# Adding x1 at the end of slot 3 of each step instead of in the middle of slot 4

## The reference

```
x1  = x + softmax(q k^T / 8) v @ Wo + bo      q = layernorm(x) @ Wq, 16 heads of 64;  k, v from the context
out = x1 + fp4(h) @ fp4(w_down)^T             h = silu(g) * u;  g, u = fp4(layernorm(x1)) @ fp4(w_gate, w_up)^T
```

## Time and profile before

| | |
|---|---|
| median of 3 runs | 984.9 us (982.71 to 985.96) |
| the profiled execution's own time | 986.75 us |
| its span, first to last instruction | 984.9 us |
| mean granted TensorE clock | 0.973 of full speed |
| PE busy | 857.0 us, 87% of the span |
| DVE busy | 757.5 us, 77% |
| ACT, POOL busy | 534.0 and 529.5 us, 54% each |
| steps between two adds of x1, away from setup | 24.7 us and 26.4 us in turn |

### The profile page before, as it was taken

How to read it: one execution, slowest core, us unless ns; L and a number is a source line. 1 busy time by engine, 2 the same in 40 slices (tenths; PEclk the granted TensorE clock), 3 DMA queues, 4 the chain that set the end, 5 groups by cost and what they waited for, 6 DMA issues and landing times.

```text
span 984.9 us, 21389 instructions
## 1 busy us (share of the span) xinstructions
PE 857.0 (87%) x6254; PEld 812.8 (83%) x6254; DVE 757.5 (77%) x2176; ACT 534.0 (54%) x1879; POOL 529.5 (54%) x677
## 2 busy tenths in 40 slices
PE   4786789999999999989989999989999999999874
PEld 3666789988888998888978888889888888888863
DVE  5857788877778888867878888876877888887762
ACT  4454455556565555556555555556555555655520
POOL 2545666554535656545554656554553656555651
PEclk9888999999999999999999999999999999999986
DMA  7101000001010000001000000001000000000000
GB/s 215 39 11 49 7 17 13 22 13 44 7 33 17 13 23 11 21 14 39 12 28 23 12 22 12 21 8 33 23 7 23 12 18 12 16 11 12 7 11 11
DMA packets 19869, 23.13 MB, mean 23 GB/s; under 512 B 2642, under 2 KB 18234, under 8 KB 19770
## 3 DMA queue, kind: packets, MB, share of 16 engines
q1 hardware_dynamic: 19770, 21.94, 7.2%
HBM read 17.74 MB, written 4.19 MB: 22 GB/s over the span
## 4 chain that ended last, share of the span: by engine, by line
PE 63%; DVE 21%; issue 8%; ACT 4%; POOL 2%; DMA 1%; DVEq 1%; SPq 0%; POOLq 0%; ACTq 0%
PE ps_g L1015 10%; PE ps_q L937 8%; PE ps_s L975 8%; PE ps_t L985 5%; PE ps_o L998 5%; PE ps_o L1000 5%; PE ps_o L999 5%; DVE negmax L782 3%; DVE pT_lo L637 3%; PE ps_m L865 3%; PE ps_g L900 3%; PE ps_m L1025 3%; PE ps_m L1027 2%; PE ps_m L1026 2%; DVE scales L667 2%
## 5 line engine op out<-in xcount | busy, mean ns | idle before, releaser
L472 POOL TENSOR_TENSOR probs<-probs,rsum 128x308 f32<-128x308 f32 x256 | 180.0, 703 | 284.2 <-DVE rsum L746 283.6
L610 ACT ACTIVATE probs<-ps_s,negmax 128x154 f32<-128x154 f32 x512 | 194.7, 386 | 229.4 <-DVE negmax L782 228.2
L998 PE MATMUL ps_o<-B_sb,pT_lo 128*128 128x256 f32 x640 | 183.6, 287 | 38.5 <-DVE x_both L804 33.9
L782 DVE TENSOR_REDUCE negmax<-ps_s 128x2 f32<-128x308 f32 x256 | 121.3, 474 | 78.4 <-PE ps_s L975 76.6
L1000 PE MATMUL ps_o<-B_sb,pT_hi 128*128 128x256 f32 x640 | 181.2, 283 | 0.0
L999 PE MATMUL ps_o<-B_sb,pT_hi 128*128 128x256 f32 x640 | 180.9, 283 | 0.0
L998 PEld LDWEIGHTS ps_o<-B_sb,pT_lo 128*128 128x128 f32 x640 | 121.7, 190 | 45.3 <-issue 42.9
L637 DVE TENSOR_TENSOR pT_lo<-ps_t,pT_hi 128x256 fp32r<-128x256 f32 (+1 forms) x256 | 122.7, 479 | 42.6 <-ACT pT_hi L514 37.4
L985 PE MATMUL ps_t<-ident,probs 128*128 128x128 f32 x640 | 115.0, 278 | 35.9 <-DVE pT_lo L637 35.3
L1015 PE MATMUL ps_g<-WGU,xqT_hi 128*128 128x352 f32 x512 | 136.6, 349 | 3.5 <-DVE B_sb L637 1.9
L514 ACT ACTIVATE pT_hi<-ps_t 128x256 fp32r<-128x256 f32 (+1 forms) x256 | 111.4, 435 | 29.1 <-PE ps_t L985 22.7
(11 more groups left out here) (149 smaller groups left out, 2236.7 us busy)
## 6 DMA issues: line engine op xcount, KB each, us to landing
xa<-in_x_dram SPq DMA_DIRECT2D x33, 128.0 KB, 2.1
xr<-in_x_dram SPq DMA_DIRECT2D x32, 128.0 KB, 2.0
out_dram<-y_xn SPq DMA_DIRECT2D x32, 128.0 KB, 1.7
W_sb<-in_L_xattn_Wk_dram SPq DMA_DIRECT2D x4, 512.0 KB, 4.4
W_sb<-in_L_xattn_Wv_dram SPq DMA_DIRECT2D x3, 512.0 KB, 3.6
probs<-in_L_xattn_Wq_dram SPq DMA_DIRECT2D x1, 1024.0 KB, 7.0
Wo_sb<-in_L_xattn_Wo_dram SPq DMA_DIRECT2D x1, 1024.0 KB, 6.6
VT<-in_ctx_dram SPq DMA_DIRECT2D x1, 384.0 KB
```

Of the source, the lines that this page charges most:

```text
L472: pool.tensor_tensor(unit, unit, rsum[:, 2 * u:2 * u + 2].unsqueeze(2) .to_broadcast([P, 2, M]), ALU.mult).then_inc(norm_p, 1)
L610: ins = act.activation(probs[:, h, 0:M], ps_s[k % 2][:, s * M:(s + 1) * M], ACT.Exp, bias=negmax[:, h:h + 1], accum_out=sums[:, h:h + 1])
L782: dve.tensor_reduce(negmax[:, 2 * k:2 * k + 2], ps_s[k % 2][:, 0:UM].rearrange("p (h m) -> p h m", h=2), AX_X, ALU.max, negate=True).then_ ...
L998: pe.matmul(ps_o[:, 0:C], lo[:, j, :], w[:, 0:C], start=first, stop=False)
```

## The change

DVE's add moves from the middle of slot 4 to the end of slot 3, with its three waits. The statistics of `x1` stay in slot 4. ACT's copy of the older `x1` to `y`, for which the add waits, moves from the end of slot 3 to the end of slot 2. PE, POOL and SP have the same instructions in the same order as before.

```diff
@@ ACT, step
                     if turn_at(t, k, 0) is not None:
                         chunk_hi(turn_at(t, k, 0))
-                    if down and k == 3:
+                    if down and k == 2:
                         at = pair - 2 + par
                         act.wait_ge(x1_v, d + 1)
                         if some(at):
...
@@ DVE, step
                     if before and k == 4:
-                        dve.wait_ge(o_mm, PAIRS * (e + 1))
-                        dve.wait_ge(xr_p, e + 1)
-                        if some(d + 1):
-                            dve.wait_ge(y_a, d + 1)
-                        elif not some(e):
-                            dve.wait_ge(raw_mm, RAW_T[3])
-                        dve.tensor_tensor(x1[1 - par], xr[1 - par][:, :], ps_o[:, 0:C], ALU.add).then_inc(x1_v, 1)
                         if some(e):
                             dve.wait_ge(xln2_a, e)
                         stats(x1[1 - par], st2, mv2, ve2, nm2, (x1_v, e + 1), ln2_v, 5 * e)
...
                         dve.wait_ge(xq_v, 6 * e + 3)
                         dve.tensor_scalar(xri[:, :], xri[:, :], TIES_DOWN, None, ALU.mult).then_inc(xq_v, 1)
+                    if before and k == 3:
+                        dve.wait_ge(o_mm, PAIRS * (e + 1))
+                        dve.wait_ge(xr_p, e + 1)
+                        if some(d + 1):
+                            dve.wait_ge(y_a, d + 1)
+                        elif not some(e):
+                            dve.wait_ge(raw_mm, RAW_T[3])
+                        dve.tensor_tensor(x1[1 - par], xr[1 - par][:, :], ps_o[:, 0:C], ALU.add).then_inc(x1_v, 1)
                     if gate and k == 6:
                         dve.wait_ge(h_v, Q * (f + 1))
```

## The result

The kernel after takes 944.5 us (median of 4 runs, 943.8 to 946.3); the kernel before, measured beside it, 983.9 us (4 runs, 982.7 to 986.0). The ratio is 0.960, with a 95% interval of 0.958 to 0.962. The forecast was 949 us in a range of 943 to 961, with 0.91 on faster: right in sign and range, 4.5 us too cautious. Of these, 1.0 is the kernel before, which the forecast took at 984.9 us; the medians differ by 39.4 us. The profiled execution took 946.30 us (span 944.4), against 986.75 us before: 40.45 us less, where 35.8 were forecast.

A forecast was written before the change was run, and what follows sets the result against it. PE (slots 2 to 5) and DVE (slot 5 to slot 1) bound the kernel in turn. Gains of 12 x 1.0 + 12 x 1.2 + 6 x 1.5 + 0.4 = 35.8 us off 984.9 gave 949 us, range 943 to 961.

The forecast's parts named there:

- The bound: PE and DVE bound the kernel in turn; PE's waits for the add of x1 make 38.5 us, 3.9% of the span.
- The add hidden: At the end of slot 3, DVE's idle of 0.30 + 0.52 + 0.26 us hides the 0.41 us add in odd steps.
- The copy at 0: ACT's copy of x1, moved a slot ahead, costs 0, with at most 0.4 us in 3 steps.
- PE's freed wait: PE's whole 1.32 us wait plus about 0.2 us goes: ahead by about 1.5 us in odd steps, 1.2 us in even.
- DVE's side of the odd step: DVE can follow by 0.52 us (statistics earlier), 0.30 (idle at slot 5's `negmax`) and up to 0.2: 1.0 us taken.
- What is late next: PE's gain lasts only as far as DVE follows; its slot 7 wait for `pT_lo` grows from 35 to 45 to 50 us.
- The clock: A half-clock stretch of PE, costing about 1.7 us, can appear or vanish; two either way are 3.4 us.
- The split of the distances: Distances between successive adds would be 23.7 and 25.2 us in turn.
- B: Rival: POOL holds the add on DVE by about 1.0 us, 9 us over 31 steps: 958 us, chance 0.05.
- C: Rival: DVE's or ACT's chain behind slot 4 takes back all but 0.44 us a step: 971 us, chance 0.13.
- D: Rival: DVE stands in slot 3 for PE's last `attend` product, each step 0.5 us longer: 1000 us, chance 0.05.
- E: Rival: the add still comes too late for PE, or another of `attend`'s waits ended last: 985 us, chance 0.04.

The follow-up runs named there:

- its version with the norm moved: Kernel after, with ACT's second layer norm moved ahead of slot 5's exponentials instead of behind them: 930.9 us (925.0 to 933.3), ratio 0.946.

## Why the prediction was right, and what was off

**The bound, right.** PE's waits for the add were on the path that sets the end: the add alone gives the whole gain, the copy alone none. It was read from two rows side by side: DVE stands idle ahead of the maximum, and PE stands idle behind it.

**The add hidden, right.** 0.67 us to spare in the odd step was forecast; one add more (0.44 us) costs nothing and three more cost 0.3 us there. In the even step, for which only the wait for `o_mm` had its room worked out (0.39 us), one more is free too.

**The copy at 0, right.** Both alone and taken back it changes no step by more than 0.04 us, but for the ones named with those runs. Where it stands only decides whether DVE's idle time is spent ahead of the add or behind it.

**PE's freed wait, right.** The 0.2 us above the bare wait (a shorter first product and its start) is borne out by the even steps: 0.99 + 0.2 was forecast, 1.19 to 1.24 us measured in 9 of 12. In "roll" steps 1.54 + 0.2 = 1.74 against 1.77 to 1.79: there I had put down the bare wait, about 1.5 us, and left the 0.2 out. That term was 0.8 us too small in all.

**DVE's side of the odd step, the mechanism right and the size too small.** This is the step that was mis-sized most: 12 x 1.0 forecast, 14.6 us measured. The working was 0.52 us (statistics earlier) + 0.30 (idle ahead of `negmax` of slot 5) + "up to 0.2". What is missing there shows beside one more row of DVE's timeline before, which stands between two of the earlier trace rows:

```profile
600.13 0.56 DVE L637 TENSOR_TENSOR hqT_lo<-ps_m,hqT_hi 128x384 fp32r<-128x384 f32 x1
```

Start to start, `negmax` of slot 4 to the statistics took 1.24 us before (596.78 to 598.02) and 0.73 after: 0.51 us. Statistics to `pT_lo` took 1.72 and now 1.50: 0.22 us. `pT_lo` to `negmax` of slot 5 took 1.25 and now 0.79: 0.46 us, where I had counted the 0.30 in the bracket. In sum 1.19 us. The bracket counts from the recorded end of the instruction before, but an instruction that needn't wait starts before that end: now `negmax` starts at 576.19, 0.47 us behind the start of `hqT_lo`, which is recorded for 0.55. So behind an idle of 0.30 stand 0.38 us or a little more; the other 0.07 us is `hqT_lo` itself, which started 0.39 us behind `pT_lo` and now starts 0.32 behind it. The Trainium skill (Perfetto Trace Analysis, Optimizing Scalar/DVE Operations) gives a DVE instruction a data-access overhead of about 60 ns on SBUF and 125 ns on PSUM, and says that the profiled latency has about twice that, since the write-acknowledgement half overlaps with the next instruction. That such starts overlap, these rows show, and their 0.08 us lies between the page's two figures.

**What is late next, right in place, the figure too high.** PE's wait for `pT_lo` was to grow to 45 to 50 us; it is 41.9. That range didn't follow from the prediction's own step, 0.7 to 1.2 us in 12 odd steps, which makes 41.3. The odd step now has 0.36 + 0.69 = 1.05 us, since DVE gained more than I gave it.

**The clock, in the bounds and not in the sum.** 1.6 us came from it. It can't be put down to the change: kernels with the same steps have the stretch in other places, and the executions of one kernel differ too (last section).

**The split of the distances, wrong without consequence.** 23.7 and 25.2 us between adds were forecast, 24.3 and 24.4 measured. The sum was forecast at 48.9 and is 48.7. The add's place within its step moved by different amounts in odd and even steps, and that enters both distances with opposite sign.

**The rivals.** B (POOL holds the add) is out: the add takes 0.41 us at 571.30, while POOL is at work on `hn`:

```profile
570.79 1.39 POOL L447 TENSOR_TENSOR hn<-hn,scales 128x704 f32<-128x704 f32 x1
```

The rule on two SBUF inputs that stood beside this step in the prediction (the Trainium skill, GPSIMD Engine Reference, Specifications) thus agrees with the trace in the new place too. C (only 0.44 us a step) is out by the table above, and the idle ahead of `negmax` of slot 5, which it would have left, is gone. D (DVE waits for PE in slot 3) shows in no row of the kernel after. E is out by the result.

## What to carry to other kernels

When one engine's instruction waits in its queue behind another that needs the waiting partner's newest work, the price isn't its own length but the whole way there and back; moving it ahead of that instruction pays even if the two engines have other waits on each other, and moving it a little earlier but still behind pays only for what it passes (some 6 us of 39 here). Estimate such an edit by the step: what the freed engine gains, what the other can follow with, the smaller of the two; and take start-to-start distances, since the idle in the brackets is too small by the overlap of starts. Then look for the next wait that ends in the same pair of engines: here the layer norm behind the exponentials, another 1.5%, which adds up with the first because it is paid in other slots.

## What the hardware showed that I had not expected

Behind an instruction that doesn't wait, DVE starts the next one 0.07 to 0.09 us before the recorded end (`hqT_lo` and `negmax` above, 0.08; the add and `rsum` in the kernel with the add alone, 596.34 + 0.42 against 596.67, 0.09). Repeats of the add that each wait for the one before start 0.45 us apart (1.35 us for three), against 0.33 from the add to the `rsum` behind it, which doesn't wait for it.

A stretch at the lower clock level (granted 0.50, which is 1.2 of 2.4 GHz) comes and goes between traced executions whose steps are otherwise equal. At steps 14 and 22 PE stands about 2 us with "issue" as the reason. In the kernel before the stretch follows at step 14. In the kernel with the copy alone it is gone there and comes at step 22, though the idle at step 14 is the longer one (PE's timeline):

```profile
435.54 0.40 PE L975 MATMUL ps_s<-K_hi,q_lo 128*128 128x308 f32 x1 [2.21 <-issue]
...
660.96 0.40 PE L975 MATMUL ps_s<-K_hi,q_lo 128*128 128x308 f32 x1 [1.93 <-issue]
```

Of the first, 435.54, the next products are at full clock. Behind the second the stretch begins some 1.5 us later (windows, columns as above):

```profile
662.40:665.60 3.20, 3.20 (x17) 3.20 (x15) 1.43 (x4) 1.47 (x6) 1.22 (x2) 0.50 0.12 41
```

Such a stretch makes its step 1.3 to 2.0 us longer, going by the distances of these two steps in the kernels run here, or 1.3 to 1.6 us when the difference of the idle ahead of it is taken off. The traced execution of the kernel after has neither stretch; that of its version with the norm moved has both, which is some 3 us of the 8.2 between this execution, 933.3 us, and the shortest of its four, 925.0. It goes by execution and not by kernel alone: 19 executions of the kernel before took 981.4 to 988.6 us, with mean granted clocks of 0.981 in the shortest and 0.971 in the longest. Each kernel was traced in one execution only. What decides it stays open: no run here varied it by itself.
